# Routed expert blocks: up weights and tokens split into heads and remainders, loads three blocks ahead, result rows weighed by GpSimd in four buffers

## The chip, the core and the metric

The kernel runs on one core of a Trainium2 chip. Five engines work side by side and meet through semaphores: TensorE (PE) multiplies matrices and transposes, VectorE (DVE) and ScalarE (ACT) work on tiles, GpSimd (POOL) does both tile work and indirect transfers, SyncE (SP) issues the other transfers. Each engine takes its instructions in the order in which they are written. The metric is the device time in microseconds (us) of one execution, lower is better.

## What is computed

The input x has 4 x 512 tokens of 512 values. A state-space layer (a scan over 16 states for each channel, driven by a context) is gated and added to x. Then a mixture of experts follows: 2 shared experts for every token, and 16 routed experts of which each token takes the best 2.

```python
aff = jax.nn.sigmoid(jnp.einsum('bsd,de->bse', x, wa))
topk_p, topk_i = jax.lax.top_k(aff, K)                      # K = 2 of E = 16
topk_p = topk_p / jnp.sum(topk_p, axis=-1, keepdims=True)
combine = jnp.sum(jax.nn.one_hot(topk_i, E, dtype=x.dtype) * topk_p[..., None], axis=2)
# _experts_all: y = gelu(x @ g + gb) * (x @ w1 + b1); y @ w2 + b2     (D = 512, F = 256)
routed = jnp.einsum('bsed,bse->bsd', _experts_all(x, rg, rgb, rw1, rb1, rw2, rb2), combine)
shared = jnp.sum(_experts_all(x, sg, sgb, sw1, sb1, sw2, sb2), axis=2)
return x + shared + routed
```

## The kernel before

The first 480 us are the scan, then come gating, normalization, the shared experts and the routing. The change is in the last stage, the routed experts, from about 693 us on. There the 4096 pairs of a token and an expert have been sorted into `NBLK` = 47 blocks of 128 rows, each with rows of one expert alone. Block j belongs to expert `blk_e[j]`, its weights lie in slot `blk_slot[j]` of four, and `blk_load[j]` says whether they have to be loaded or are there already. `ids` and `row_w` hold the token and the weight of each row.

What happens to a block, in order, with the semaphore that each step raises:

- GpSimd fetches 128 rows of tokens (`fetch`, L534, xg_0 to xg_3). SyncE loads up weights (128 x 2048, 1 MB) and down weights (0.5 MB) into their slots (`load`, L366), two blocks ahead for up.
- TensorE transposes the tokens (L1550, xgt_ready); ScalarE copies them from PSUM to SBUF (L816, xgt_copied).
- TensorE multiplies by the up weights: four fp32 products of 512 columns, gate and linear half at once (L1559, h_ready). The trace has two rows of matmul for each.
- VectorE adds the bias (L1227, hb_ready), ScalarE applies gelu to one half (L820, hg_ready), VectorE multiplies the halves (L1233, hy_ready).
- TensorE transposes the result (L1567, hyt_ready), ScalarE copies it (L825), TensorE multiplies by the down weights (L1576, o_ready).
- VectorE adds the output bias (L1240, yb_ready), ScalarE weighs the rows (L831, `y_sb`, two buffers, y_ready), and GpSimd adds them to the output in DRAM by an indirect transfer (L560, y_even and y_odd when it has landed). Where a block starts a new expert, GpSimd first waits until the addition ahead of it has landed.

The steps of several blocks are interleaved by hand. `step(j)` on TensorE does up of j+1, transposed hidden of j, tokens of j+3, down of j-1; on VectorE bias j, product j, output bias j-2; on ScalarE gelu j, weighing j-2, transposed hidden j, tokens j+3. The steps of the first blocks and the last are written out, those between run in a hardware loop of four blocks. Where an operand depends on the expert or the slot, the engine first reads the number from SBUF into a register (`value_load`, TENSOR_LOAD in the order of instructions).

In the shared experts each fp32 operand is split already: a head rounded to the type fp32r and a remainder, and `split_product` (L1418 to L1420) makes three single-pass products for each pair of operands (head by head, head by remainder, remainder by head).

Results of the shared experts and x are added up in `acc`, and GpSimd stores its 16 tiles to the output (`store_base`, L523; early_stored for tiles 0 to 7, late_stored for 8 to 15) before the routed rows are added to them. `acc_again` is a name for the memory of `acc` that later steps may reuse; `mem` and `split` name one region in the same way.

## Time and profile before

| | before |
|---|---|
| median of 3 runs | 987.9 us (987.62 to 990.82) |
| profiled execution, time | 990.75 us |
| its span | 989.0 us |
| TensorE matmul, busy | 820.5 us, 83% of the span |
| TensorE weight load, busy | 562.8 us, 57% |
| VectorE, busy | 636.4 us, 64% |
| ScalarE, busy | 512.0 us, 52% |
| GpSimd, busy | 554.4 us, 56% |
| routed stage, first transpose to last up product | 693.4 to 962.6 us |

Busy shares are averages over stages with different limits: the scan keeps VectorE and GpSimd busy, the routed stage TensorE. Of the routed stage the reader should look at stretches of their own, and at which wait ends last there. Times below are counted from the start of the span.

### The profile page before, as it was taken

Reading aid. Unit: us, or ns where it says so; the run is one execution under the profiler, and the core shown is the slowest. Engines: PE = TensorE matmul, PEld = TensorE weight load, DVE = VectorE, ACT = ScalarE, POOL = GpSimd, SP = SyncE. Lnnn points to the kernel's source line nnn. Section 1 sums busy time; section 2 is a strip of 40 time slices with the busy share of each in tenths; the row PEclk is TensorE's granted clock in tenths of the full one; section 3 lists DMA queues with packets and bytes.
Section 4 is the critical chain, followed back from the end, with each engine's and each line's share of the span. In section 5 each row is a group of like instructions: output and inputs, shape, how many; then the busy total and the mean of one; then the engine's idle time right before and its main releaser. Section 6 shows DMA issues by size and latency. Waiting matters only on the chain.

```text
span 989.0 us, 14660 instructions
## 1 busy us (share of the span) xinstructions
PE 820.5 (83%) x4030; PEld 562.8 (57%) x4031; DVE 636.4 (64%) x669; ACT 512.0 (52%) x831; POOL 554.4 (56%) x483
## 2 busy tenths in 40 slices
PE   6987487677777777777588998989999999999991
PEld 2323476666666766666566776777445444544440
DVE  4858899989999998898877675542223332333230
ACT  3578498778888897898124321201233333333330
POOL 2211199889999899999555244020344444444331
PEclk9966699989999898998799998989999999999996
DMA  5010031112132112110311112046867877787533
GB/s 157 0 48 1 25 104 43 43 43 60 49 106 65 58 50 84 45 44 1 115 50 49 43 38 81 12 168 270 288 153 200 209 181 208 205 233 157 86 43 42
DMA packets 32421, 95.40 MB, mean 96 GB/s; under 512 B 5088, under 2 KB 5216, under 8 KB 29040
## 3 DMA queue, kind: packets, MB, share of 16 engines
q1 hardware_dynamic: 20400, 65.37, 19.4%
q0 software_dynamic: 11968, 29.37, 14.8%
q8 instruction: 28, 0.46, 0.2%
q14 instruction: 25, 0.20, 0.1%
HBM read 122.11 MB, written 21.36 MB: 145 GB/s over the span
## 4 chain that ended last, share of the span: by engine, by line
PE 59%; DVE 18%; issue 8%; POOL 7%; ACT 4%; DMA 2%; DVEq 0%; SPq 0%; POOLq 0%; ACTq 0%
PE ps L1559 16%; DVE r L953 11%; PE ps L1576 8%; POOL r L464 6%; PE ps L1364 5%; PE ps L1341 5%; PE ps L1418 5%; PE ps L1420 4%; PE ps L1419 4%; PE ps L1273 3%; PE ps L1550 2%; DVE r L962 2%; PE ps L1281 2%; PE ps L1296 1%; ACT mem L687 1%
## 5 line engine op out<-in xcount | busy, mean ns | idle before, releaser
L953 DVE TENSOR_TENSOR_SCAN r<-r,ps 128x1024 f32<-128x1024 f32 x128 | 286.0, 2271 | 24.2 <-PE ps L1364 15.5
L464 POOL TENSOR_TENSOR r<-r,mem 128x512 f32<-128x512 f32 x224 | 288.6, 1318 | 12.2 <-DVE r L953 6.8
L1341 PE MATMUL ps<-ident,mem 128*128 128x128 f32 x1024 | 145.5, 289 | 74.3 <-DVE r L953 56.7
L675 ACT ACTIVATE r<-mem,nega 128x511 f32<-128x511 f32 x256 | 168.7, 713 | 37.6 <-DVE r L953 37.6
L1341 PEld LDWEIGHTS ps<-ident,mem 128*128 128x128 f32 x1024 | 119.6, 148 | 97.5 <-issue 80.7
L1559 PE MATMUL ps<-r,mem 128*128 x376 | 169.1, 592 | 0.4 <-ACT mem L816 0.4
L1364 PE MATMUL ps<-ident,r 128*128 128x128 f32 x1024 | 145.3, 283 | 16.9 <-DVE r L962 10.4
L560 POOL DMA_INDIRECT out<-sg,ids x47 | 74.5, 1586 | 144.2 <-DMA out<-sg,ids 113.4
L1364 PEld LDWEIGHTS ps<-ident,r 128*128 128x128 f32 x1024 | 120.6, 145 | 25.1 <-DVE r L962 13.6
L687 ACT ACTIVATE mem<-mem,bc 128x512 f32<-128x512 f32 x192 | 124.7, 712 | 14.0 <-PE ps L1341 13.1
L1559 PEld LDWEIGHTS ps<-r,mem 128*128 128x128 f32 x376 | 71.2, 190 | 89.1 <-issue 89.1
L1227 DVE TENSOR_TENSOR mem<-ps,mem 128x512 f32<-128x512 f32 x47 | 32.5, 692 | 124.3 <-PE ps L1559 124.3
L1576 PE MATMUL ps<-mem 128*128 x188 | 88.5, 594 | 0.9 <-DVE sb_sb L1240 0.7
L1418 PE MATMUL ps<-split 128*128 128x512 f32 x192 | 78.5, 409 | 7.1 <-DVE split L1008 3.4
L831 ACT ACTIVATE sg<-sb_sb,row_w 128x512 f32<-128x512 f32 x47 | 33.9, 722 | 96.9 <-DVE sb_sb L1240 88.9
L456 POOL TENSOR_SCALAR mem<-mem,bc 128x512 f32<-128x512 f32 x64 | 53.7, 839 | 45.6 <-PE ps L1307 26.4
L1420 PE MATMUL ps<-split 128*128 128x512 f32 x192 | 76.4, 398 | 0.0
L1419 PE MATMUL ps<-split 128*128 128x512 f32 x192 | 76.3, 398 | 0.0
L748 ACT ACTIVATE sg<-ps,sbg_sb 128x512 f32<-128x512 f32 x16 | 11.0, 688 | 101.6 <-PE ps L1420 101.6
L534 POOL DMA_INDIRECT r<-xn_scratch,ids x47 | 48.6, 1034 | 24.0 <-issue 13.8
L825 ACT COPY mem<-ps 128x256 f32<-128x256 f32 x47 | 17.5, 372 | 79.2 <-PE ps L1567 73.0
L962 DVE TENSOR_TENSOR r<-r,mem 128x512 f32<-128x512 f32 x32 | 56.9, 1777 | 0.0
(172 smaller groups left out, 1000.8 us busy)
## 6 DMA issues: line engine op xcount, KB each, us to landing
r<-in_r_up SPq DMA_DIRECT2D x47, 1024.0 KB
mem<-in_r_down SPq DMA_DIRECT2D x47, 512.0 KB
mem<-cm_rows SPq DMA_DIRECT2D x64, 256.0 KB, 3.3
mem<-in_r_b SPq DMA_DIRECT2D x4, 2048.0 KB, 11.7
r<-in_x SPq DMA_DIRECT2D x4, 1024.0 KB, 4.9
xn_scratch<-r SPq DMA_DIRECT2D x16, 256.0 KB, 2.3
out<-acc POOLq DMA_DIRECT2D x16, 256.0 KB, 2.7
mem<-in_ctx_t SPq DMA_DIRECT2D x4, 512.0 KB, 8.3
```

Of the source, the lines that this page charges most:

```text
L464: pool.tensor_tensor(state[:, k % 2, ec], state[:, k % 2, ec], cb[:, k % CROWS], ALU.mult).then_inc(s["weighed_p"], 1)
L675: act.activation(decay[:, k % 2, ec, 1:L], delta[:, b, ec, 1:L], ACT.Exp, scale=nega[:, ec, n:n + 1]).then_inc(s["decay_ready"], 1)
L687: act.activation(dbu_t[:, k % 2, lt], du_t[:, t], ACT.Copy, scale=bc[:, t, DR + k % DS:DR + k % DS + 1]).then_inc(s["dbut_made_a"], 1)
L953: dve.tensor_tensor_scan(state[:, half, ec:ec + 2].rearrange("p e l -> p (e l)"), decay[:, half, ec:ec + 2].rearrange("p e l -> p (e l)"), ...
L962: dve.tensor_tensor(state[:, k % 2, EC - 1], state[:, k % 2, EC - 1], cb[:, k % CROWS], ALU.mult).then_inc(s["weighed_v"], 1)
L1341: mm = pe.transpose(ps[:, ec, lt * P:(lt + 1) * P], dbu_t[:, k % 2, lt, ec * P:(ec + 1) * P], ident[:])
L1364: mm = pe.matmul(ps[:, Y_BANK + lt, ec * P:(ec + 1) * P], state[:, k % 2, ec, lt * P:(lt + 1) * P], ident[:], is_transpose=True, start=Fal ...
L1418: pe.matmul(to, one_pass(l_head), one_pass(r_head), start=(first and i == 0), stop=False)
L1419: pe.matmul(to, one_pass(l_head), one_pass(r_rest), start=False, stop=False)
L1420: mm = pe.matmul(to, one_pass(l_rest), one_pass(r_head), start=False, stop=(last and i == n - 1))
L1559: mm = pe.matmul(ps[:, r % 2], xgt[:, r % 2, kc * P:(kc + 1) * P], up_weights(slot_j, kc), start=(kc == 0), stop=(kc == KC - 1))
L1576: mm = pe.matmul(ps[:, 6 + r % 2], hyt[:, r % 2, fc * P:(fc + 1) * P], down_weights(slot_j, fc), start=(fc == 0), stop=(fc == FC - 1))
```

## The change

Only the routed stage changes, in five places:

- ScalarE copies the up weights of each block from their slot to `up_head`, rounded (`weight_head`), and VectorE makes the remainder (`weight_rest`, a subtraction of 128 x 2048). The buffers, two of each, lie in `acc_again`.
- The transposed tokens are split likewise: ScalarE's copy is rounded, VectorE subtracts it from PSUM (`token_rest`).
- TensorE's `up` makes 12 single-pass products from the four parts instead of four fp32 ones. It waits for xgr_made and upr_made, VectorE's remainders.
- Up weights are loaded three blocks ahead (`AHEAD`), and a slot is free when its remainder is made, not when its product is.
- ScalarE's weighing is gone. VectorE writes the output bias sum straight into one of four buffers `y_sb`, and GpSimd multiplies it by `row_w` in place before its indirect addition. ScalarE's tokens come two blocks ahead instead of three.

```diff
+AHEAD = 3
-        xgt = view(mem, LATE_AT, 2, D)
+        xgt = view(split, LATE_AT, 2, D)
-        y_sb = sg
-        yb = sb2_sb
+        y_sb = (sg[:, 0], sg[:, 1], sb2_sb[:, 0], sb2_sb[:, 1])
+        up_head = view(acc_again, 0, 2, 2 * UP)[:, :, 0:UP]
+        up_rest = view(acc_again, 0, 2, 2 * UP)[:, :, UP:2 * UP]
+        xgt_rest = view(blk_val_again, 0, 2, D)
...
             def load_up(j, r):
                 if not isinstance(j, int) or j >= SLOTS:
-                    wait_apart(sp, s["h_ready"], j - SLOTS + 1)
+                    wait_apart(sp, s["upr_made"], j - SLOTS + 1)
...
                 for r in range(RING):
                     load_down(RING * jj + r, r)
-                    load_up(RING * jj + r + 2, (r + 2) % RING)
+                    load_up(RING * jj + r + AHEAD, (r + AHEAD) % RING)
...
-                pool.wait_ge(s["y_ready"], j + 1)
+                pool.wait_ge(s["yb_ready"], j + 1)
+                pool.tensor_scalar(y_sb[j % RING], y_sb[j % RING], row_w[:, j:j + 1], 1.0, ALU.mult, ALU.mult).then_inc(
+                    s["y_ready"], 1)
+                if j >= 2:
+                    pool.wait_ge(s["y_odd" if j % 2 else "y_even"], 16 * (j // 2))
...
             def turn_tokens(j, half):
                 act.wait_ge(s["xgt_ready"], j + 1)
                 since(act, s["h_ready"], j - 1)
-                act.copy(xgt[:, half], ps[:, 4 + half]).then_inc(s["xgt_copied"], 1)
+                act.copy(one_pass(xgt[:, half]), ps[:, 4 + half]).then_inc(s["xgt_copied"], 1)
+            def weight_head(j, r, round_):
+                slot_j = act.value_load(blk_slot[0:1, ds(j, 1)], min_val=0, max_val=SLOTS - 1)
+                act.wait_ge(s[f"up_{r}"], 16 * (round_ + 1))
+                since(act, s["h_ready"], j - 1)
+                act.copy(one_pass(up_head[:, r % 2]), up_weights(slot_j)).then_inc(s["uph_made"], 1)
...
             def step(j, round_, r):
+                if not isinstance(j, int) or j + 2 < NBLK:
+                    weight_head(j + 2, (r + 2) % RING, round_ + (r + 2) // RING)
+                    turn_tokens(j + 2, r % 2)
                 hidden_gate(j, r % 2)
-                if not isinstance(j, int) or j >= 2:
-                    block_result(j - 2, r % 2, (RING // 2) * round_ + (r - 2) // 2)
                 turn_hidden(j, r % 2)
-                if not isinstance(j, int) or j + 3 < NBLK:
-                    turn_tokens(j + 3, (r + 1) % 2)
+            act.wait_ge(s["blocks_ready"], 3)
+            act.wait_ge(s["early_stored"], 16 * NT // 2)
+            weight_head(0, 0, 0)
             act.wait_ge(s["so_ready"], NT)
             turn_tokens(0, 0)
             turn_tokens(1, 1)
-            turn_tokens(2, 0)
+            act.wait_ge(s["late_stored"], 16 * NT // 2)
+            weight_head(1, 1, 0)
...
-            add_shared(3, every)
+            def weight_rest(j, half):
+                slot_j = dve.value_load(blk_slot[0:1, ds(j, 1)], min_val=0, max_val=SLOTS - 1)
+                dve.wait_ge(s["uph_made"], j + 1)
+                dve.tensor_tensor(one_pass(up_rest[:, half]), up_weights(slot_j), up_head[:, half],
+                                  ALU.subtract).then_inc(s["upr_made"], 1)
+            def token_rest(j, half):
+                dve.wait_ge(s["xgt_copied"], j + 1)
+                dve.tensor_tensor(one_pass(xgt_rest[:, half]), ps[:, 4 + half], xgt[:, half],
+                                  ALU.subtract).then_inc(s["xgr_made"], 1)
...
-            def step(j, r):
+            def step(j, round_, r):
                 hidden_bias(j, r % 2)
+                if not isinstance(j, int) or 0 < j < NBLK - 1:
+                    token_rest(j + 1, (r + 1) % 2)
+                if not isinstance(j, int) or j >= 2:
+                    add_bias(j - 2, (r - 2) % RING, round_ + (r - 2) // RING)
                 hidden(j, r % 2)
-                if not isinstance(j, int) or j >= 2:
-                    add_bias(j - 2, r % 2)
+                if not isinstance(j, int) or j + 2 < NBLK:
+                    weight_rest(j + 2, r % 2)
+            weight_rest(0, 0)
+            add_shared(3, every)
+            token_rest(0, 0)
+            token_rest(1, 1)
+            weight_rest(1, 1)
...
-            def up(j, r, round_):
-                slot_j = pe.value_load(blk_slot[0:1, ds(j, 1)], min_val=0, max_val=SLOTS - 1)
-                pe.wait_ge(s["xgt_copied"], j + 1)
-                pe.wait_ge(s[f"up_{r}"], 16 * (round_ + 1))
+            def up(j, r):
+                pe.wait_ge(s["xgr_made"], j + 1)
+                pe.wait_ge(s["upr_made"], j + 1)
                 since(pe, s["hb_ready"], j - 1)
-                for kc in range(KC):
-                    mm = pe.matmul(ps[:, r % 2], xgt[:, r % 2, kc * P:(kc + 1) * P], up_weights(slot_j, kc),
-                                   start=(kc == 0), stop=(kc == KC - 1))
-                mm.then_inc(s["h_ready"], 1)
+                split_product(ps[:, r % 2], [(xgt[:, r % 2, kc * P:(kc + 1) * P], xgt_rest[:, r % 2, kc * P:(kc + 1) * P],
+                                              up_head[:, r % 2, kc * 2 * F:(kc + 1) * 2 * F],
+                                              up_rest[:, r % 2, kc * 2 * F:(kc + 1) * 2 * F])
+                                             for kc in range(KC)]).then_inc(s["h_ready"], 1)
```

How the order of instructions moves is shown at two places. The first is ScalarE in the loop of the routed blocks, one block before the change. L825 is the copy of the transposed hidden part, L816 the tokens, L820 the gelu, L831 the weighing; "waits" lists the semaphores.

```order
L820 ACTIVATE mem<-mem 128x256 [waits hb_ready]
L285 REGISTER_ALU [waits yb_ready]
L831 ISA [waits y_even]
L831 ACTIVATE sg<-sb_sb,row_w 128x512
L825 COPY mem<-ps 128x256 [waits o_ready,hyt_ready]
```

And the same place after it. Line numbers are those of the changed kernel: L831 is now the read of the slot number, L834 the weight heads, L827 the tokens, L838 the gelu, L843 the transposed hidden part.

```order
L831 ISA
L831 TENSOR_LOAD blk_slot
L831 ISA x2
L834 ISA [waits h_ready,up_3]
L834 COPY acc_again<-r 128x2048
L825 REGISTER_ALU
L827 CAST split<-ps 128x512 [waits h_ready,xgt_ready]
L838 ACTIVATE mem<-mem 128x256 [waits hb_ready]
L843 COPY mem<-ps 128x256 [waits o_ready,hyt_ready]
```

The weighing is gone; a read of the slot number and the copy of 2048 columns stand at the start of a block, behind the copy L843 of the block before and ahead of tokens and gelu.

The second place is VectorE in the same loop, one block before the change. L1227 is the bias, L1233 the product, L1240 the output bias; TENSOR_LOAD of `blk_e` reads the expert's number.

```order
L1227 ISA [waits hy_ready,hg_ready,h_ready]
L1227 TENSOR_TENSOR mem<-ps,mem 128x512
L1233 TENSOR_TENSOR mem<-mem 128x256 [waits hb_ready,hg_ready,hyt_ready]
L1218 TENSOR_LOAD blk_e
L1218 ISA x2
L1240 ISA [waits o_ready,y_ready]
L1240 TENSOR_TENSOR sb_sb<-ps,mem 128x512
```

After the change, in its line numbers, L1249 is the bias, L1241 the token remainder, L1263 the output bias, L1255 the product and L1236 the weight remainder.

```order
L1249 ISA [waits hy_ready,hg_ready,h_ready]
L1249 TENSOR_TENSOR mem<-ps,mem 128x512
L1241 TENSOR_TENSOR blk_val_again<-ps,split 128x512 [waits xgt_copied]
L1230 TENSOR_LOAD blk_e
L1230 ISA x2
L1263 ISA [waits y_odd,o_ready]
L1263 TENSOR_TENSOR sg<-ps,mem 128x512
L1255 TENSOR_TENSOR mem<-mem 128x256 [waits hb_ready,hg_ready,hyt_ready]
L1234 ISA
L1234 TENSOR_LOAD blk_slot
L1234 ISA x2
L1236 ISA [waits uph_made]
L1236 TENSOR_TENSOR acc_again<-r,acc_again 128x2048
```

The token remainder stands behind the bias, the output bias has moved ahead of the product, and a third read of a register and the weight remainder stand behind the product.

## Rows read from the trace of the kernel before

**Rows 1.** Chain that ended last, routed stage: start us, us, what.
```profile
698.58 0.44 PE ps L1550 x4
...
703.40 3.60 DMA r<-xn_scratch,ids
...
709.88 3.43 PE ps L1559 x8
...
713.31 0.22 PE ps L1567 x2
...
959.16 3.45 PE ps L1559 x8
...
967.75 4.60 DMA out<-sg,ids
```

**Rows 2.** Busy time by stretch; the last three columns: TensorE clock, DMA share, GB/s.
```profile
680.00:685.00 5.00, 3.92 (x12) 2.83 (x11) 1.63 (x3) 0.62 (x1) 0.59 (x1) 0.73 0.99 419
...
850.00:900.00 50.00, 50.00 (x158) 25.00 (x157) 15.35 (x26) 17.20 (x35) 24.63 (x19) 1.00 0.82 215
```

**Rows 3.** Timeline of one routed block: start us, us, engine, line, operation.
```profile
800.26 0.38 PE L1567 MATMUL ps<-ident,mem 128*128 128x128 f32 x2
...
800.68 0.37 ACT L825 COPY mem<-ps 128x256 f32<-128x256 f32 x1 [1.62 <-PE ps L1567]
...
801.19 0.58 ACT L816 COPY mem<-ps 128x512 f32<-128x512 f32 x1
...
801.67 0.42 ACT L820 ACTIVATE mem<-mem 128x256 f32<-128x256 f32 x1
...
802.18 0.43 DVE L1233 TENSOR_TENSOR mem<-mem 128x256 f32<-128x256 f32 x1 [0.90 <-ACT mem L820]
...
803.04 0.69 DVE L1240 TENSOR_TENSOR sb_sb<-ps,mem 128x512 f32<-128x512 f32 x1 [0.43 <-issue]
...
813.72 0.48 DVE L1233 TENSOR_TENSOR mem<-mem 128x256 f32<-128x256 f32 x1 [0.68 <-ACT mem L820]
...
814.92 0.69 DVE L1240 TENSOR_TENSOR sb_sb<-ps,mem 128x512 f32<-128x512 f32 x1 [0.72 <-PE ps L1576]
```

**Rows 4.** Timeline of TensorE in the shared experts, single-pass products.
```profile
672.02 0.39 PE L1418 MATMUL ps<-split 128*128 128x512 f32 x1
...
674.74 0.39 PE L1418 MATMUL ps<-split 128*128 128x512 f32 x1
...
679.63 0.50 PE L1418 MATMUL ps<-split 128*128 128x512 f32 x1 [0.65 <-DVE split L1014]
...
679.97 0.39 PE L1419 MATMUL ps<-split 128*128 128x512 f32 x1
```

**Rows 5.** Timeline of VectorE: subtractions and products of 2048 columns, remainders of 512.
```profile
104.55 2.28 DVE L885 TENSOR_TENSOR mem<-mem,r 128x2048 f32<-128x2048 f32 x1
...
106.75 1.27 DVE L919 COPY mem<-ps 128x512 f32<-128x512 f32 x2
...
530.09 2.48 DVE L1008 TENSOR_TENSOR split<-ps,split 128x512 fp32r<-128x512 f32 x4 [0.46 <-ACT split L741]
```

**Rows 6.** Groups by line and shape, ScalarE and GpSimd: count, busy us, mean ns.
```profile
L635 ACT ACTIVATE r<-r 128x2048 f32<-128x2048 f32 x4 | 7.7, 1919 | 1.7 <-DVE r L879 1.7
...
L456 POOL TENSOR_SCALAR mem<-mem,bc 128x512 f32<-128x512 f32 x64 | 53.7, 839 | 45.6 <-PE ps L1307 26.4 <-PE ps L1341 19.2
```

**Rows 7.** Timelines of GpSimd and VectorE in the scan, two long operations.
```profile
97.65 4.83 POOL L456 TENSOR_SCALAR mem<-mem,bc 128x512 f32<-128x512 f32 x1
...
170.05 5.40 DVE L962 TENSOR_TENSOR r<-r,mem 128x512 f32<-128x512 f32 x1
```

**Rows 8.** Timeline of GpSimd, its fifth fetch.
```profile
703.40 0.99 POOL L534 DMA_INDIRECT r<-xn_scratch,ids  x1 [9.41 <-PE ps L1550]
```

**Rows 9.** DMA queues, 693.5 to 702.6 us: packets, MB, share.
```profile
q0 software_dynamic: 201, 0.63, 17.2%
```

**Rows 10.** DMA queues, 702.6 to 704.9 us.
```profile
q1 hardware_dynamic: 106, 0.84, 92.1%
```

More of the change, by code:

```diff
@@ L219, in bass_xattn_scan_moe_kernel @@
         row_hot = view(r0, 8192, 2, GROUP, P)
-        blk_val = sb("blk_val", [P, 2, GROUP, 2 * NBLK])
+        with ExitStack() as listing:
+            blk_val = listing.enter_context(nc.sbuf_tensor("blk_val", [P, 2, GROUP, 2 * NBLK], F32))
+        blk_val_again = sb("blk_val_again", [P, 2 * GROUP * 2 * NBLK])
         half_i = sb("half_i", [P, 2 * ((NBLK + 3) // 2)], I32)
@@ L286, in wait_apart, with up_weights @@
             eng.sem_inc(S["waits_passed"], 1)
[L288 to L290 removed]
+        def up_weights(slot_j):
+            return up_w[:, bass.ds(slot_j, 1)].rearrange("p o n -> p (o n)")
         def down_weights(slot_j, fc):
@@ L390, in _ @@
             sp.dma_start(b2_all[:, 0:E // 2], r_b2[0:E // 2].unsqueeze(0).to_broadcast([P, E // 2, D])).then_inc(s["loaded_b2"], 16)
-            for j in range(2, RING):
-                load_up(j + 2, (j + 2) % RING)
+            for j in range(1, RING):
+                load_up(j + AHEAD, (j + AHEAD) % RING)
             with sp.Fori(1, (NBLK - 2) // RING) as jj:
@@ L852, in _ @@
                 step(j, j // RING, j % RING)
-            for j in range(NBLK - 2, NBLK):
-                block_result(j, j % 2, j // 2)
         @block.vector
@@ L1547, in turn_tokens @@
                 pe.wait_ge(s[f"xg_{r}"], 16 * (round_ + 1))
-                since(pe, s["xgt_copied"], j - 1)
+                since(pe, s["xgr_made"], j - 1)
                 for kc in range(KC):
@@ L1590, in _ @@
             turn_tokens(1, 1, 0)
-            up(0, 0, 0)
+            up(0, 0)
             turn_tokens(2, 2, 0)
@@ L1600, in _ @@
             last = NBLK - 1
-            up(last, last % RING, last // RING)
+            up(last, last % RING)
             turn_hidden(last - 1, (last - 1) % RING)
```

37 lines of the change are left out of this document (16 added, 21 removed).

## The prediction

> **What bounds the kernel now.** I read the chain that ended last first. From 713 us on it is TensorE alone: up products (L1559), transposes (L1567, L1550), down products (L1576), block after block, with no wait between them [rows 1]. Call E(j) the moment at which the up products of block j end, which is where the transposes behind them start. E(3) is 713.31; the last up products, of block 46, start at 959.16 and take 3.45, so E(46) is 962.61 [rows 1]. That is 249.3 us for 43 blocks, 5.80 us each. In 850 to 900 us TensorE is busy for all of the stretch at the full clock, while VectorE works 31%, ScalarE 34% and GpSimd 49% of it [rows 2]. So anything that shortens TensorE's work in a block is gained, until another engine or a loop through several engines is longer than TensorE's work.
>
> **TensorE's share of the change.** Up goes from 3.43 us of fp32 products [rows 1] to 12 single-pass products. The same form runs in the shared experts: from 672.02 to 674.74 are twelve of them, 2.72 us, 0.227 each at the full clock [rows 4]. That takes 0.71 off, and TensorE's work in a block becomes 5.80 - 0.71 = 5.09 us.
>
> **What it adds elsewhere, per block.** ScalarE copies 2048 columns of weights: the nearest rows are four activations of the same shape, 1.92 us [rows 6]; it loses the 0.72 us of weighing. VectorE subtracts the same 2048 columns, 2.28 us as at 104.55 [rows 5], and 512 columns of tokens from PSUM, 0.69 or less: four such operations in a row took 2.48 us [rows 5]. VectorE's busy time is then 3 x 0.69 + 0.43 + 2.28 = 4.78 us, ScalarE's 1.92 + 0.58 + 0.42 + 0.37 = 3.29. Both are under 5.09, so by busy time alone nothing stands against a gain of 0.71 us a block. GpSimd gets the weighing, 0.84 us by the mean of its like, L456 [rows 6], and has the room. Loading three blocks ahead costs nothing: a slot is free once the remainders are made, and four blocks of lead hold either way.
>
> **The loop that busy time doesn't show.** The new steps stand in series through four engines. ScalarE works in program order: transposed hidden of block j-1, weight heads of j+2, tokens of j+2, gelu of j. VectorE: bias j, token remainder j+1, output bias j-2, hidden product j, weight remainder j+2. TensorE's up of block j+2 waits for the token remainder of j+2, which stands behind bias j+1, which stands behind the weight remainder of j+2. Followed from E(j), with starts read from one block [rows 3]:
> - transposes end, ScalarE starts its copy: 800.26 to 800.68, 0.42
> - that copy's start to the weight heads. A slot number has to be read into a register in between, and the order of instructions shows the read behind the copy. ScalarE has no such read before the change; VectorE has one between L1233 and L1240, and there the starts lie 0.86 (802.18, 803.04) to 1.20 (813.72, 814.92) apart [rows 3]. I take 0.95
> - weight heads: 1.92 [rows 6] less the 0.1 by which ScalarE's operations overlap (801.19 + 0.58 against 801.67 [rows 3]): 1.80 rounded
> - tokens to gelu 0.48, gelu to hidden product 0.51 [rows 3]
> - hidden product to weight remainder, again with a read of the slot, 0.95
> - weight remainder to the next VectorE operation: 104.55 to 106.75, 2.20 [rows 5]
> - bias j+1 0.60 and token remainder 0.68, from the pace of the four [rows 5]
> - TensorE starts 0.05 after it; the first product after a wait takes 0.34 instead of 0.23 (679.63 to 679.97) [rows 4], then the rest of 2.72: 2.88
>
> The sum is 11.47 us from E(j) to E(j+2), so 5.74 us a block, although no engine works more than 5.09. With the reads at 0.86 it is 5.65, at 1.20 5.99. So of the 0.71 us that TensorE saves, 0.06 is left. In the change the weighing went to GpSimd, whose operation starts when output bias j-2 ends. That is about 3.5 us after E(j), and it reaches into the start of hidden product j at about 4.1. I allow 0.1 us a loop for that.
>
> The Trainium skill (VectorE: DVE Perf Modes, The DRAIN you can't avoid) says that the next VectorE operation doesn't start until the pipe is empty. Here it starts 0.08 us before the end of the one ahead (104.55 + 2.28 against 106.75) [rows 5], so the trace disagrees; by that rule the three back-to-back steps of the loop would be 0.25 us longer and a block 0.12.
>
> **The start.** The weights' heads and remainders lie where the result rows lay, and the second half of it may be written only when the last eight tiles of rows are stored. GpSimd waits for the same stores ahead of its fifth fetch, which starts at 703.40 [rows 8]; its queue still had 201 packets between 693.5 and 702.6 [rows 9], and from there to 704.9 only SyncE's queue had any [rows 10]. So the stores land at about 702.6. Now ScalarE waits for them before the heads of block 1. From there: heads 703.5 to 705.4, remainder to 707.7, up of block 1 from 707.8. TensorE has then been idle since the transposes of block 2, about 699.0 [rows 1]. After shorter pauses the clock was at 0.73 in 680 to 685, against 1.00 later [rows 2]: part of that stretch ran at 1.2 GHz. I take eight products at half the clock, so up takes 4.3 us and E(1) is 712.1. One loop on, E(3) is 723.6 instead of 713.31: 10.3 us lost. Before, this stretch had a stall of its own (3.60 us for a fetch at 703.40 [rows 1]), which is in the 713.31.
>
> **The sum.** E(45) = 723.6 + 21 x 11.47 = 964.5. The even blocks run by a loop of their own: weight remainder of 2 to 712.2, bias 1 at 712.4, token remainder to 713.7, E(2) = 716.6, and E(46) = 716.6 + 22 x 11.47 = 968.9, at least 5.09 behind E(45): 969.6. With 0.1 a loop for the weighing 971.8. That is 9.2 later than 962.61. Behind E(46) the result of block 44 waits for ScalarE no longer; I take off 0.5 and no more, since the last additions to the output each wait for the landing of the one ahead, 4.60 us at 967.75 [rows 1], either way. So +8.7 us. The profiled execution took 990.75 us (span 989.0), 2.85 over the median of 987.9. It would become 999.4, the median 996.6. I say 996.
>
> **Rivals.**
> - TensorE stays the bound (0.10). The reads of registers overlap or ScalarE runs ahead, and the loop is under 10.2 us. For it: both engines are idle half of the time. Against it: the sum above, which would have to be 1.3 us too long. E(46) = 723.6 + 43 x 5.09 = 942.5, 20 us earlier; median 967.
> - The loop is 10.6 to 11.2 us, or the start costs less (stores earlier, clock not lowered) (0.21). E(46) lies between 952 and 964: median 977 to 990, half of it under 985.
> - The shared port (0.16). GpSimd and VectorE shut each other out: a weighing-like operation of GpSimd (L456) took 4.83 us at 97.65, beside VectorE's operations with two SBUF inputs, and a 512-column product of VectorE (L962) took 5.40 at 170.05, beside GpSimd [rows 7]. The rule behind it is in the Trainium skill (GPSIMD Engine Reference, Key points): contention with VectorE instructions that have two SBUF inputs. Hidden product and weight remainder are such, the other three read PSUM. If each loop waits once for a whole 0.84, a block costs (11.47 + 0.84) / 2 = 6.16 us, and E(46) is 723.6 + 43 x 6.16 = 988.5, 26 later; median 1013; for half of that wait 1004. It decides from 0.1 us a loop on.
> - The forecast (0.53): 991 to 1003.
>
> **How the numbers follow.** No change is told from one here only beyond 0.3%, 3 us. Faster than 985: the first rival and half of the second, 0.20. Within 3 us: the rest of the second, 0.11, and the low edge of the forecast, 0.02. Slower 0.67. The range leaves out most of the first rival and the top of the third: 978 to 1011.
>
> **What the changed profile would show.** Twelve products of 0.23 us for a block; TensorE idle about 0.6 us ahead of each up, released by VectorE's token remainder; ScalarE's heads of 1.9 us about 1.4 us after E(j); VectorE's weight remainder about 4.9 after it; E(3) near 723 and an idle stretch of 8 us ahead of up 1. I am wrong if TensorE shows no idle time (first rival), if the gap between hidden product and weight remainder is under 0.3 us, if weight remainders take over 2.6 or hidden products over 0.6 (third), or if the heads of block 1 start well before 703.

## The result, and the profile after

The changed kernel takes 1023.4 us (median of four executions) against 987.8 before: 1.034 times as long, 95% interval 1.025 to 1.042. (The ratios in this document compare means and leave out executions of a slower state that turns up now and then, here the one of 1033.64 us.) The forecast was 996, the range 978 to 1011. The profiled execution after took 1020.27 us, its span is 1018.4. The parts ahead of the routed stage, whose code the change leaves alone, come out differently from one execution to the next: the last addition to a base row (L1029 before, L1041 after) starts at 692.47 us before and at 684.43 after, and between 683 and 705 us in the kernels below. The difference is there when the scan ends, near 470 to 490 us, and it goes mostly with one group: the scan's 32 products of VectorE (`r<-r,mem`, 128x512, the L962 of [rows 7]) take 1.45 us in the mean after, 1.78 before, and 2.19 to 2.22 in the three kernels below in which that addition comes last, behind 701 us. The order is not strict: in gate_first it is 1.86 us with the addition at 685.9. Why the products take so long in some executions is open. So profiles are compared here by three parts of the routed stage, read from the timeline: **start**, from the start of that last addition to E(3); **blocks**, E(3) to E(46); **tail**, E(46) to the end of the span. E(j) is the start of the transposes behind the up products of block j, as in the prediction.

```
                          start    blocks (each)    tail   stage
before                     20.7    249.3 (5.80)     26.6   296.5
predicted                  31.1    248.2 (5.77)     26.1   305.4
after                      31.7    259.4 (6.03)     42.8   334.0
```

The stage is 37.5 us longer, of which the prediction had 8.9 (8.7 in its own sum, where E(46) of before is read 0.2 later). Its start was right, the blocks are 11 us longer than forecast, the tail 17.

**Start**, timeline of the kernel after (columns as in [rows 3]; of the lines in between these are the ones that matter), then windows of it (columns as in [rows 2]):

```profile
684.43 0.69 DVE L1041 TENSOR_TENSOR acc<-ps,acc 128x512 f32<-128x512 f32 x1 [2.03 <-PE ps L1452]
...
695.63 3.70 ACT L834 CAST acc_again<-r 128x2048 fp32r x2 [8.46 <-DMA out<-acc]
...
697.67 2.29 DVE L1236 TENSOR_TENSOR acc_again<-r,acc_again 128x2048 fp32r<-128x2048 f32 x1 [9.66 <-ACT acc_again L834]
...
700.11 0.77 PE L1450 MATMUL ps<-acc_again,split 128*128 128x512 f32 x1 [7.59 <-DVE acc_again L1236]
...
705.10 0.38 PE L1598 MATMUL ps<-ident,mem 128*128 128x128 f32 x2
```

```profile
700.00:705.00 5.00, 4.89 (x12) 3.92 (x13) 3.28 (x3) 0.42 (x1) 0.78 (x1) 0.52 0.19 52
```

ScalarE's heads of block 1 wait 8.46 us for the stores (`out<-acc`), VectorE's remainder waits for the heads, TensorE 7.59 us for the remainder. This is the chain of the prediction: the heads start 11.2 us behind the start of the last base addition, where 11.0 was forecast. Up of block 1 then takes 5.0 us (700.11 to 705.10) instead of the 4.3 I took. The granted clock is 0.52 in 700 to 705, so nearly all of the stretch runs at 1.2 GHz: the first eleven products start 0.42 to 0.56 us apart, where 0.23 is the distance at 2.4 GHz.

**Blocks.** These are the starts of TensorE's transposes, E(3) to E(7):

```profile
716.15 0.38 PE L1598 MATMUL ps<-ident,mem 128*128 128x128 f32 x2
721.29 0.38 PE L1598 MATMUL ps<-ident,mem 128*128 128x128 f32 x2
727.63 0.38 PE L1598 MATMUL ps<-ident,mem 128*128 128x128 f32 x2
732.79 0.38 PE L1598 MATMUL ps<-ident,mem 128*128 128x128 f32 x2
739.32 0.38 PE L1598 MATMUL ps<-ident,mem 128*128 128x128 f32 x2
```

Two blocks take 11.48, then 11.50, then 11.69 us, so the loop of 11.47 is there, but the pace doesn't stay. The next lines are waits of TensorE and VectorE in 715 to 975 us (us in total, times, longest):

```profile
PEld ps L1450 <- DVE blk_val_again L1241: 50.9, 43, 2.0
...
DVE sg L1263 <- DMA out<-sg,ids: 8.8, 7, 3.9
...
DVE sb_sb L1263 <- DMA out<-sb_sb,ids: 7.8, 5, 2.6
```

The first is the loop's wait for token remainders. The other two are new: VectorE's output bias of block j waits until the addition of block j-4 has landed, 16.6 us in all. The longest of these waits belong to one stall: an addition took 10.81 us from issue to landing, and GpSimd and then VectorE waited (the first line is from the chain, the second from the timeline).

```profile
839.53 10.81 DMA out<-sb_sb,ids
...
859.14 0.69 DVE L1263 TENSOR_TENSOR sg<-ps,mem 128x512 f32<-128x512 f32 x1 [3.86 <-DMA out<-sg,ids]
```

The three blocks from E(25), 845.14, to E(28), 867.95, take 22.8 us, and the other forty 5.92 each. So about 5 of the 11 us over the forecast were lost here. The other 6 are spread over all blocks. The chain that ended last, in 730 to 940 us, was TensorE alone before [rows 1]; now it holds no TensorE at all:

```profile
by line: issue 30.9%; DMA out<-sb_sb,ids 21.0%; POOL r L540 18.3%; POOL sg L560 8.7%; POOL out L571 8.4%; POOL sb_sb L560 6.1%; DMA out<-sg,ids 5.2%; POOLq L568 2.2%; POOLq L292 0.5%
```

It is GpSimd's chain: scaling (L560), register read (L568), addition (L571) and its landing, fetch (L540). Here is one round of it on the timeline, with VectorE's weight remainder (L1236) beside it:

```profile
820.01 0.85 POOL L560 TENSOR_SCALAR sg<-sg,row_w 128x512 f32<-128x512 f32 x1
820.88 2.29 DVE L1236 TENSOR_TENSOR acc_again<-r,acc_again 128x2048 fp32r<-128x2048 f32 x1 [0.58 <-issue]
821.71 2.96 POOL L571 DMA_INDIRECT out<-sg,ids  x1 [0.84 <-POOL sg L560]
824.98 1.01 POOL L540 DMA_INDIRECT r<-xn_scratch,ids  x1 [0.30 <-issue]
...
826.01 0.85 POOL L560 TENSOR_SCALAR sg<-sg,row_w 128x512 f32<-128x512 f32 x1
826.41 2.60 DVE L1236 TENSOR_TENSOR acc_again<-r,acc_again 128x2048 fp32r<-128x2048 f32 x1
827.70 2.80 POOL L571 DMA_INDIRECT out<-sg,ids  x1 [0.84 <-POOL sg L560]
```

From addition to addition it takes 5.99 us: 2.96 + 0.30 + 1.01 + 0.02 + 0.85 + 0.84 (times and idle times, in order), and no wait for a landing is in it. An addition took 1.59 us before (mean of 34 in 750 to 950 us). Here it is 2.96, and it ends at 824.67, 1.50 behind the end of the remainder at 823.17; the next one ends at 830.50, 1.49 behind the end of the remainder at 829.01. This is no accident of two. Between E(3) and E(46) eleven additions start 0.11 us or more into a remainder. They take from 1.91 to 3.69 us, and every one ends 1.50 us behind the end of the remainder, nearly the whole length of an addition that is left alone. In the same way 16 fetches end 0.88 to 0.89 us behind it, and eleven scalings 0.54 to 0.56. Additions that start ahead of a remainder take 1.60 to 1.86. So an instruction of GpSimd that starts under a remainder does next to nothing until VectorE has finished. The groups of GpSimd's instructions in 750 to 950 us (busy us, mean ns | idle before, releaser):

```profile
L540 POOL DMA_INDIRECT r<-xn_scratch,ids x31 | 49.2, 1587 | 9.5 <-issue 9.2 <-DMA out<-sg,ids 0.3
L571 POOL DMA_INDIRECT out<-sb_sb,ids x16 | 32.8, 2053 | 20.0 <-POOL sb_sb L560 9.6 <-DMA out<-sb_sb,ids 7.6 <-DMA out<-sg,ids 2.9
L571 POOL DMA_INDIRECT out<-sg,ids x16 | 32.4, 2023 | 20.6 <-POOL sg L560 11.0 <-DMA out<-sb_sb,ids 8.5 <-issue 1.0
L560 POOL TENSOR_SCALAR sg<-sg,row_w 128x512 f32<-128x512 f32 x16 | 20.4, 1273 | 0.6
L560 POOL TENSOR_SCALAR sb_sb<-sb_sb,row_w 128x512 f32<-128x512 f32 x16 | 16.1, 1006 | 0.6
```

**Tail.** This is the same chain from E(46), 975.59, on:

```profile
978.85 5.10 DMA out<-sg,ids
...
984.84 4.79 DMA out<-sb_sb,ids
...
990.52 4.94 DMA out<-sb_sb,ids
...
996.36 4.83 DMA out<-sg,ids
...
1002.08 4.67 DMA out<-sg,ids
...
1007.65 1.59 POOL out L571
```

Six additions are issued behind E(46), each waiting for the landing of the one ahead, 5.6 to 6.0 us apart. Before there were three, the first at 967.75 [rows 1], and one more that started with E(46) itself, at 962.45. Three more additions at 5.6 us or more are about the 16 us by which the tail is longer. GpSimd was three blocks behind when TensorE ended.

### The profile page after: what moved, and what is told of

Read it like the earlier page. It is cut to its first block, busy times and chain, and to the rows that moved or that the text cites. A ratio compares the mean times of both kernels' runs of the same rounds, so it can differ in the third digit from the quotient of the medians.

```text
span 1018.4 us, 15319 instructions
## 1 busy us (share of the span) xinstructions
PE 808.2 (79%) x4218; PEld 591.9 (58%) x4219; DVE 761.9 (75%) x763; ACT 563.0 (55%) x832; POOL 648.3 (64%) x530
## 4 chain that ended last, share of the span: by engine, by line
PE 33%; DVE 18%; POOL 16%; issue 15%; DMA 12%; ACT 4%; POOLq 1%; DVEq 0%; SPq 0%; ACTq 0%
DVE r L965 11%; DMA out<-sb_sb,ids 6%; POOL r L470 5%; PE ps L1373 5%; PE ps L1450 5%; DMA out<-sg,ids 5%; PE ps L1396 5%; PE ps L1451 5%; PE ps L1452 5%; POOL r L540 4%; PE ps L1305 2%; POOL out L571 2%; POOL sg L560 2%; PE ps L1313 2%; PE ps L1328 1%
## 5 line engine op out<-in xcount | busy, mean ns | idle before, releaser
L1373 PE MATMUL ps<-ident,mem 128*128 128x128 f32 x1024 | 141.1, 283 | 72.7 <-DVE r L965 51.2
L1373 PEld LDWEIGHTS ps<-ident,mem 128*128 128x128 f32 x1024 | 115.5, 145 | 95.8 <-issue 70.1
L1236 DVE TENSOR_TENSOR acc_again<-r,acc_again 128x2048 fp32r<-128x2048 f32 x47 | 110.7, 2356 | 29.6 <-issue 18.1
L834 ACT CAST acc_again<-r 128x2048 fp32r x47 | 89.2, 1901 | 36.5 <-issue 28.1
L1450 PE MATMUL ps<-acc_again,split 128*128 128x512 f32 x188 | 81.8, 435 | 28.1 <-DVE blk_val_again L1241 20.2
L1607 PE MATMUL ps<-mem 128*128 x188 | 93.2, 621 | 3.5 <-ACT mem L843 3.4
L540 POOL DMA_INDIRECT r<-xn_scratch,ids x47 | 70.8, 1507 | 32.1 <-issue 13.2
L843 ACT COPY mem<-ps 128x256 f32<-128x256 f32 x47 | 17.5, 372 | 111.9 <-PE ps L1598 108.2
L1450 PEld LDWEIGHTS ps<-acc_again,split 128*128 128x128 f32 x188 | 36.3, 193 | 68.9 <-DVE blk_val_again L1241 54.7
L1452 PE MATMUL ps<-acc_again,blk_val_again 128*128 128x512 f32 x188 | 75.5, 402 | 0.0
L1451 PE MATMUL ps<-acc_again,split 128*128 128x512 f32 x188 | 75.4, 401 | 0.0
L571 POOL DMA_INDIRECT out<-sg,ids x24 | 48.0, 2001 | 41.8 <-DMA out<-sb_sb,ids 16.5
```

Source lines behind the costliest of these rows:

```text
L540: pool.indirect_dma_start(out=xg[:, j % RING], out_offset=None, in_=xn_dram, in_offset=bass.IndirectOffsetOnAxis(ids[:, j:j + 1], 0)).then ...
L1236: dve.tensor_tensor(one_pass(up_rest[:, half]), up_weights(slot_j), up_head[:, half], ALU.subtract).then_inc(s["upr_made"], 1)
L1373: mm = pe.transpose(ps[:, ec, lt * P:(lt + 1) * P], dbu_t[:, k % 2, lt, ec * P:(ec + 1) * P], ident[:])
L1450: pe.matmul(to, one_pass(l_head), one_pass(r_head), start=(first and i == 0), stop=False)
L1451: pe.matmul(to, one_pass(l_head), one_pass(r_rest), start=False, stop=False)
L1452: mm = pe.matmul(to, one_pass(l_rest), one_pass(r_head), start=False, stop=(last and i == n - 1))
```

## Experiments

The experiments set two theories against each other. Theory A: GpSimd's work for a block, made longer by the scaling and stretched by VectorE, has become the bound (A1: the stretching decides; A2: four steps in series are too long without it). Theory B: the loop through the other three engines is 6.0 by itself. The table has the three parts of each profile, and the times. Each ratio is to the kernel before as it ran beside that experiment (medians of 990.1 to 992.9 us), so kernels of different groups are compared by the ratio and not by the time.

```
kernel        start   blocks (each)   tail   stage   time, median   ratio to before (95%)
after_again    32.2   257.4 (5.99)    43.2   332.8    1020.2        1.032  (1.025-1.039)
act_weighs     32.2   253.1 (5.89)    27.8   313.1    1008.0        1.015  (1.009-1.021)
rest_psum      31.8   245.5 (5.71)    26.8   304.0    1001.5        1.012  (1.006-1.019)
fold           32.2   250.7 (5.83)    26.2   309.1    1013.1        1.021  (1.016-1.026)
weigh_only     21.5   249.3 (5.80)    27.2   298.0     991.0        1.002  (0.997-1.007)
gate_first     31.6   255.1 (5.93)    40.0   326.7    1028.4        1.038  (1.029-1.047)
start_fix      22.8   255.9 (5.95)    42.6   321.3    1015.6        1.023  (1.016-1.031)
best1          23.7   250.4 (5.82)    26.0   300.1     994.1        1.002  (0.999-1.005)
best2          22.6   243.9 (5.67)    28.6   295.1     987.6        0.992  (0.988-0.997)
best3          22.7   238.6 (5.55)    28.8   290.0     988.5        0.993  (0.987-0.998)
best4          22.9   232.6 (5.41)    29.3   284.8     980.8        0.992  (0.989-0.996)
best5          22.5   232.8 (5.41)    39.5   294.8     992.7        1.002  (0.997-1.006)
```

**after_again**, no edit.

> The changed kernel once more, nothing edited, as the measure for the three beside it. Every theory expects 1015 to 1027 us. In its trace the stage should again be made of three parts: about 31 us from the last addition to a base row (L1029's) to E(3), the moment at which the up products of block 3 end; about 6.0 us a block from E(3) to E(46); and some 40 us or more from E(46) to the end, with about six additions to the output issued behind E(46).

All three parts came again within 2 us. Each part is read from one profiled execution, so differences of 2 us between kernels are not told apart here.

**act_weighs**

```diff
-                pool.tensor_scalar(y_sb[j % RING], y_sb[j % RING], row_w[:, j:j + 1], 1.0, ALU.mult, ALU.mult).then_inc(
+                act.activation(y_sb[r], y_sb[r], ACT.Copy, scale=row_w[:, ds(j, 1)]).then_inc(s["y_ready"], 1)
```

> The changed kernel with the weighing back on ScalarE, in the same four buffers; nothing else. Theory A (GpSimd's serial work for a block, scaling, register read, addition, fetch, about 6 us, is longer than the loop through the other engines): without the scaling GpSimd needs 4.7 us, the blocks fall to the loop's 5.75, only three additions stand behind E(46), the tail is 25 to 30 us. Time 997 to 1006. Theory B (the loop through ScalarE, VectorE and TensorE is 6.0 by itself, GpSimd only follows): blocks stay at 6.0, 1008 to 1016 with a shorter tail at most. Theory C (the four buffers or loads three ahead do the harm): no change, 1015 to 1027.

The tail is back at 27.8 us, as theory A has it, but a block takes 5.89, 0.14 longer than it said, and the time of 1008.0 lies above its range and at the edge of theory B's. Theory B had room for a shorter tail, so this run alone doesn't decide between the two; the next one does. Theory C falls: the four buffers and the loads three ahead were kept.

**rest_psum**

```diff
-                dve.tensor_tensor(one_pass(up_rest[:, half]), up_weights(slot_j), up_head[:, half],
-                                  ALU.subtract).then_inc(s["upr_made"], 1)
+                    dve.tensor_tensor(one_pass(up_rest[:, half]).rearrange("p (c n) -> p c n", c=KC),
+                                      up_head[:, half].rearrange("p (c n) -> p c n", c=KC),
+                                      ps[:, 4 + half, 0:UP // KC].unsqueeze(1).to_broadcast([P, KC, UP // KC]),
+                                      ALU.subtract).then_inc(s["upr_made"], 1)
```

> The changed kernel, but from block 2 on the weights' remainder is computed with the second operand read from PSUM (a 512-column bank, read four times) in place of the loaded weights in SBUF: as many columns, one SBUF input instead of two. The remainders are then wrong in value. Theory A1 (GpSimd's instructions are stretched because VectorE's operation with two SBUF inputs shuts it out): scalings fall from a mean of 1.27 us to about 0.85, fetches from 1.57 to about 1.05, additions from 1.98 to about 1.6, GpSimd's work in a block to under 5 us, time 995 to 1006 with a tail under 32. Theory A2 (GpSimd is too long only because four steps stand in series, and the port has no part): all durations on GpSimd stay within 0.1, time 1015 to 1027.

The kernel still has the scaling on GpSimd, and VectorE's operation takes 2.29 us. These are its groups on GpSimd, same stretch and columns:

```profile
L540 POOL DMA_INDIRECT r<-xn_scratch,ids x34 | 34.4, 1012 | 10.4 <-issue 10.1 <-DMA out<-sg,ids 0.3
L571 POOL DMA_INDIRECT out<-sg,ids x18 | 29.2, 1624 | 33.3 <-DMA out<-sb_sb,ids 16.6 <-DMA out<-sg,ids 8.0 <-POOL sg L560 6.0
...
L560 POOL TENSOR_SCALAR sb_sb<-sb_sb,row_w 128x512 f32<-128x512 f32 x18 | 13.0, 724 | 7.3 <-DVE sb_sb L1269 6.8
```

The fetch goes from 1.59 to 1.01, the addition from 2.04 to 1.62, the scaling from 1.14 to 0.72 (means over both buffers): 1.4 us a block less on GpSimd, from one input of a VectorE operation. No addition takes over 1.67 us, wherever it starts. The tail is 26.8, the scaling now waits for VectorE, and no VectorE operation waits for a landing. A1 holds, A2 falls. So does theory B: the loop through the other three engines has the same steps here, and it isn't 6.0. With GpSimd out of the way a block takes 5.71 us, and the prediction's sum for the loop was 5.74. The Trainium skill (GPSIMD Engine Reference, Key points) has the rule behind it, contention with VectorE instructions that have two SBUF inputs. The trace agrees, and it shows the same for the instructions with which GpSimd issues indirect transfers.

**fold**

```diff
+                dve.scalar_tensor_tensor(out=hy[:, half], in0=hg[:, half], scalar=row_w[:, ds(j, 1)],
+                                         in1=hb[:, half, F:2 * F], op0=ALU.mult, op1=ALU.mult).then_inc(s["hy_ready"], 1)
...
+                dve.scalar_tensor_tensor(out=y_sb[r], in0=tile(b2_all, e), scalar=row_w[:, ds(j, 1)],
+                                         in1=ps[:, 6 + r % 2], op0=ALU.mult, op1=ALU.add).then_inc(s["yb_ready"], 1)
```

> The changed kernel, with the weighing folded into two VectorE operations of the same length: the hidden product also takes the row's weight, and the output bias is taken times that weight, so that no engine has a weighing of its own and GpSimd has only fetches and additions. Theory A (GpSimd's chain): 996 to 1005, blocks at 5.7 to 5.8 us, tail 25 to 30 us, the additions and fetches still stretched beside the weights' remainder. Theory B (loop of the other three is 6.0 by itself): 1008 to 1016. If fused operations of VectorE with a scalar from SBUF are slower than the plain ones by 0.2 us each, a block is 0.2 longer, and it is 1005 to 1012.

No engine has a weighing of its own, the tail is 26.2 and a block 5.83. The fused operations take 0.06 us longer than the plain ones, 0.484 and 0.743 against 0.426 and 0.686 in act_weighs (means in 750 to 950 us), not 0.2. The time, 1013, is above the 996 to 1005 expected. The stage (309.1) is 13 us over that of before, and the rest lies ahead of it, where this kernel has the code of the others. Against after_again the stage is 24 us shorter and the time only 7.

**weigh_only**, the kernel before with GpSimd's lines of the change.

```diff
-                act.activation(y_sb[:, half], yb[:, half], ACT.Copy, scale=row_w[:, ds(j, 1)])
+                pool.tensor_scalar(y_sb[j % RING], y_sb[j % RING], row_w[:, j:j + 1], 1.0, ALU.mult, ALU.mult).then_inc(
```

> The kernel before, with only the weighing moved to GpSimd and the result in four buffers; up products in fp32 as before, no heads and no remainders. Theory A1 (GpSimd's work becomes too long because VectorE's weight remainder shuts it out): without the remainder GpSimd's scaling takes about 0.72 us, its addition 1.6, its fetch 1.05, under 5 us with the register read, so TensorE stays the bound at 5.80 us a block, and the time is that of before, 985 to 994. Theory A2 (the scaling in series is too much by itself): blocks of 5.9 to 6.1 us and a tail of 35 us or more, 1000 to 1015.

A1 again: the time is the same within the interval, and blocks take 5.80. (Its profiled execution was 13 us over its median, 12 of them ahead of the stage.) So the scaling is harmless alone; it takes the weight remainder beside it.

**gate_first**

```diff
+                hidden_gate(j, r % 2)
                 if not isinstance(j, int) or j + 2 < NBLK:
                     weight_head(j + 2, (r + 2) % RING, round_ + (r + 2) // RING)
                     turn_tokens(j + 2, r % 2)
-                hidden_gate(j, r % 2)
```

> The changed kernel, but ScalarE does the gelu of block j ahead of the weight heads and tokens of block j+2 instead of behind them. By the sum of the prediction that takes about 1.1 us off the loop of two blocks (10.2 to 10.4 us in place of 11.47). Theory A (GpSimd's work for a block, stretched, is 5.9 to 6.1 us and is the bound): blocks stay at 5.8 to 6.0 us, and what is won from E(3) to E(46) comes back in a longer tail; time 1010 to 1024. Theory B (the loop through ScalarE, VectorE and TensorE is the bound and GpSimd only follows it): blocks at 5.2 to 5.4 us and 990 to 1000.

A block takes 5.93 us and the tail 40, as theory A has it; the time of 1028.4 is above its range. There is a second reason why the blocks did not get shorter, see best1.

**start_fix**

```diff
             turn_tokens(1, 1)
-            act.wait_ge(s["late_stored"], 16 * NT // 2)
-            weight_head(1, 1, 0)
...
+                    if isinstance(j, int) and j == 1:
+                        act.wait_ge(s["late_stored"], 16 * NT // 2)
                     weight_head(j + 2, (r + 2) % RING, round_ + (r + 2) // RING)
...
+                    for kc in range(KC):
+                        mm = pe.matmul(ps[:, r % 2], y_sb[3][:, kc * P:(kc + 1) * P],
+                                       up_weights(slot_j)[:, kc * 2 * F:(kc + 1) * 2 * F],
+                                       start=(kc == 0), stop=(kc == KC - 1))
```

> The changed kernel, but block 1 alone is multiplied in fp32 as before the change, from a full copy of its tokens, so that no weight head or remainder of it is made, and ScalarE waits for the last stores of the rows only ahead of the head of block 3. The prediction's start term (about 10 us lost because heads of block 1 wait for the late stores): the time from the last addition to a base row to E(3) falls from 31 us to 20 to 22, the rest stays, time 1010 to 1017. If the start is lost to something else (the fetch of block 4 behind the same stores, or a low clock): it falls by less than 3 us, time 1017 to 1024.

The start falls by 8.9 us, to 22.8 where 20 to 22 was expected, and the time of 1015.6 is in the range. So the start term is shown: the wait of block 1's heads for the stores costs 9 of the 11 us.

**best1**: fold, gate_first and start_fix together, and the fetch of block 4 no longer waits for the stores.

> Four edits together: weighing folded into VectorE's two operations, gelu ahead of the weight heads on ScalarE, block 1 in fp32, and GpSimd waits for the stores of the rows only ahead of the first addition, so that the fetch of block 4 does not wait for them. If GpSimd without the scaling keeps up (theory A), the start is 18 to 21 us, a block 5.2 to 5.5 us, the tail 26 to 30: 962 to 977. If GpSimd's stretched fetch and addition or the landing of additions still bind at 5.7 to 5.8: 982 to 990.

Theory A's 5.2 to 5.5 us a block did not come, and 994.1 us is above both ranges. The timeline shows a loop I had not worked out (rows of VectorE and ScalarE, block after block the same):

```profile
799.87 2.29 DVE L1239 TENSOR_TENSOR acc_again<-r,acc_again 128x2048 fp32r<-128x2048 f32 x1 [1.29 <-ACT acc_again L837]
...
802.08 0.68 DVE L1253 TENSOR_TENSOR mem<-ps,mem 128x512 f32<-128x512 f32 x1
...
802.79 0.42 ACT L841 ACTIVATE mem<-mem 128x256 f32<-128x256 f32 x1 [1.32 <-DVE mem L1253]
...
803.56 1.91 ACT L837 CAST acc_again<-r 128x2048 fp32r x1 [0.35 <-issue]
...
805.62 2.29 DVE L1239 TENSOR_TENSOR acc_again<-r,acc_again 128x2048 fp32r<-128x2048 f32 x1 [1.15 <-ACT acc_again L837]
```

With the gelu ahead, the heads of block j+2 wait for the bias of block j, which stands behind the weight remainder of j+1: one block per turn, 5.75 us. So the "about 1.1 us off the loop" expected for gate_first was wrong. The two orders come out alike, 5.82 a block here and 5.83 in fold, which has the order of the change.

**best2**: best1 with ScalarE's order of the change again, and

```diff
                 hidden_gate(j, r % 2)
+                if more:
+                    slot_j = slot_of(j + 3)
                 turn_hidden(j, r % 2)
...
+                if more:
+                    slot_j = slot_of(j + 2)
                 hidden(j, r % 2)
```

> As the kernel of four edits, but ScalarE's order is that of the change again (weight heads ahead of the gelu), and the slot number is read into a register earlier: on ScalarE ahead of the wait for the transposed hidden rows, on VectorE ahead of the hidden product. The prediction's loop of two blocks loses the two reads that it counts (about 0.45 us each of the 0.95 steps): 10.5 to 10.7 us, 5.25 to 5.35 a block. If the loop bounds: E(3) to E(46) 226 to 232 us, start 21 to 23, tail 26 to 29, time 966 to 975. If GpSimd (fetch, register read, addition, stretched) bounds at 5.7 or more: 245 to 250 from E(3) to E(46) or a tail over 35, 985 to 992.

Early pairs of blocks take 10.5 to 10.6 us as expected, but the mean of a block is 5.67, and the time of 987.6 misses the 966 to 975. In the chain, 740 to 752 us, SyncE's queue (SPq) has taken over (L369 to L372 are 52% of it in the whole loop, 716 to 948 us):

```profile
by line: issue 25.1%; SPq L369 21.6%; SPq L370 21.1%; SPq L372 15.7%; SPq L371 15.3%; SPq L403 1.1%; SPq L292 0.6%
```

Its issues of weight loads in the timeline:

```profile
742.14 0.36 SPq L372 DMA_DIRECT2D mem<-in_r_down  x1
745.59 0.35 SPq L372 DMA_DIRECT2D r<-in_r_up  x1
748.11 0.09 SPq L372 DMA_DIRECT2D mem<-in_r_down  x1
750.59 0.09 SPq L372 DMA_DIRECT2D r<-in_r_up  x1
```

It takes 2.5 to 3.5 us from load to load, and a block has two loads. L369 to L371 read expert, "new or not" and slot into registers; that is most of it.

**best3**: best2, heads and remainder of a block in two halves of 1024 columns.

> As the one above, and the weights of a block are split in two halves of 1024 columns, so that VectorE's first half of the remainder runs beside ScalarE's second half of the heads. The loop loses another 0.95 us less two short overheads of 0.1 to 0.2: 9.7 to 9.9 us, so that TensorE's own work (5.09 us and some 0.1 of restart) becomes the bound: 5.1 to 5.25 a block, 219 to 226 us from E(3) to E(46), time 958 to 970. If GpSimd bounds, no gain over the one above, and a longer tail.

The stage is 5 us shorter and the time no different. E(3) to E(46) takes 238.6 us where 219 to 226 was expected, and the time of 988.5 is far above the 958 to 970. SyncE's reads and the landing of additions are in the chain.

**best4** and **best5**: best3 and best2, with SyncE reading the numbers of a block once for both loads. With it the up weights are loaded two blocks ahead again, and ahead of the down weights.

```diff
+                        known.append(numbers(j + 2))
+                        load_up(j + 2, (r + 2) % RING, known[r + 2])
+                    load_down(j, r, known[r])
-                    load_down(RING * jj + r, r)
-                    load_up(RING * jj + r + AHEAD, (r + AHEAD) % RING)
```

> As the kernel with early reads and halves, but SyncE reads the three numbers of a block (expert, new or not, slot) once for its two loads, up two blocks ahead, instead of once for each load; at the start of each round of four it reads two blocks again, so 18 reads in four blocks instead of 24. In the two kernels ahead SyncE issues its two loads of a block 5.3 to 5.8 us apart, one after the other without a wait. If SyncE's reads bound them: blocks fall from 5.55 to 5.15 to 5.3 us, 222 to 228 from E(3) to E(46), time 968 to 980. If the additions, which land some 5.5 us after their issue and wait for each other, are the bound: 235 to 240 as before, or a tail longer by what is gained, 984 to 992.

> The same edit of SyncE on the kernel with early reads, without halves. If SyncE's reads bound that one: 226 to 230 from E(3) to E(46) (the loop of 5.25 to 5.35 us), time 972 to 982. If the additions bound: 240 to 245 as before, 984 to 992.

Both fall in blocks, to 5.41: 6.0 us less than best3, 11.1 less than best2, so SyncE's reads did bound them. Both are still up to 0.1 us a block above the expected range, which is left open, and the times are above theirs, by 1 us in best4 and 11 in best5. For best5 gives all that it gains back in the tail. The next lines are GpSimd's fetches and additions, best4 first, then best5:

```profile
L560 POOL DMA_INDIRECT r<-xn_scratch,ids x34 | 39.5, 1163 | 10.4 <-issue 8.8 <-DMA out<-sb_sb,ids 0.6 <-DMA out<-sg,ids 0.6
L589 POOL DMA_INDIRECT out<-sb_sb,ids x19 | 34.6, 1821 | 45.8 <-DMA out<-sg,ids 24.8 <-DMA out<-sb_sb,ids 16.4 <-issue 4.6
```

```profile
L560 POOL DMA_INDIRECT r<-xn_scratch,ids x32 | 50.2, 1569 | 9.8 <-issue 7.9 <-DMA out<-sb_sb,ids 0.9 <-DVE sb_sb L1293 0.9
L589 POOL DMA_INDIRECT out<-sb_sb,ids x17 | 37.5, 2203 | 31.5 <-DMA out<-sg,ids 13.6 <-DMA out<-sb_sb,ids 10.6 <-DVE sb_sb L1293 4.6
```

The kernels differ only in whether heads and remainder are one operation each (VectorE's of 2.29 us) or two (of 1.22). With one, a fetch is stretched to 1.57 us, and six additions stand behind E(46); with two it is 1.16, and four do. best4 has the shortest stage, 284.8 us, and takes 0.992 (0.989 to 0.996) of before; best2 and best3 come out at the same ratio.

## Why the prediction was wrong, step by step

- **Twelve products of 0.23, the loop, 11.47 us.** This was right. Early pairs took 11.48 to 11.69, and rest_psum, with GpSimd out of the way, runs at 5.71 a block against 5.74.
- **The start, 10.3 us.** This was right: 11.0 measured, and start_fix takes 8.9 of them back. Up of block 1 was 0.7 longer than I took. Of that 0.2 is a slip in the sum, since eight products at half the clock and four at the full one are 8 x 0.454 + 4 x 0.227 = 4.5 us and not 4.3; the rest is that nearly all ran at the lower clock.
- **"GpSimd gets the weighing, 0.84 us by the mean of its like, L456 [rows 6], and has the room."** This step failed, and with it the sum: GpSimd's round was priced at nothing. I had GpSimd's busy share from [rows 2] (49%), and left out what lies between its instructions: 0.84 us from scaling to addition, 0.30 to the fetch, and landings. 1.06 + 0.30 + 1.59 + 0.84 + 0.72 is 4.5 us at the lengths without contention, which would have fitted (weigh_only, rest_psum). Stretched under the weight remainder it is 6.0, more than the 5.74 of the loop. So GpSimd falls behind until VectorE waits for its additions, which gives blocks of 6.03 and three more additions in the tail: 11.2 and 16.7 us over the forecast, of the 28.6 that the stage is over it.
- **The shared port.** It was the right rival with the wrong victim. I priced one wait of 0.84 us a loop on the scaling or the hidden product, 1013 us in all. What is stretched is all that GpSimd does: the fetch by 0.58 in the mean, addition and scaling by 0.42 each, and single additions by 2.1 (to 3.69), since the remainder of 2.29 us lies over one of them in nearly every block. The signs that the prediction named for this rival came only in part: remainders took 2.36 us in the mean and 2.77 at most, hidden products 0.53 in the mean and 1.02 at most. The rows at hand showed 5 us stalls between the two engines [rows 7], and I tried them only on the instruction that the change moved, not on those already there.
- **The tail, "I take off 0.5 and no more, since the last additions to the output each wait for the landing of the one ahead".** The landings behind one another were right, and they are what made the backlog dear: GpSimd came to E(46) three additions further behind, each 5.6 us or more, and the tail is 16.2 us longer than before. I had assumed that the backlog is the same in both kernels.
- **"I allow 0.1 us a loop for that."** Two blocks took 12.07 us in the mean where 11.57 was forecast, so the loop came out 0.6 longer than its 11.47 and not 0.1. Of these 0.6 about 0.24 is the one stall behind the addition at 839.53 (5 us in 21.5 loops). The delay of the hidden product by the scaling, for which the 0.1 stood, is there: it starts 0.80 us behind the gelu in the mean of E(3) to E(46), and 0.51 in rest_psum.
- **The pipe that has to be empty.** The prediction sets a sentence of the Trainium skill (VectorE: DVE Perf Modes, The DRAIN you can't avoid) against the rows. The same section adds that an operation which is not held starts earlier, so the 0.08 us of overlap don't contradict it. In the kernel after, too, bias starts 2.21 us behind the start of a remainder of 2.29.

Taking the scaling off GpSimd (act_weighs, fold) is enough to bring the tail back; that leaves the start and blocks of 5.8 to 5.9, 13 to 17 us over before in the stage. The split itself gains nothing on this loop, as forecast. A block still takes 0.12 us longer in fold and 0.18 in act_weighs than in rest_psum. Part of it lies ahead of the weight remainder, where VectorE idles 0.55, 0.60 and 0.38 us in the three (means in 750 to 950 us, released by no wait that the profile shows). Why is left open; fold and act_weighs keep the operation with two SBUF inputs.

## What to carry to other kernels

When work is moved to an engine that is half idle, add up its whole round for one block in series, with register reads, gaps and landings, and then stretch every instruction in it, old ones too, to the end of the longest operation with two SBUF inputs that VectorE may run beside it. An engine that falls behind by a fraction of a block every time shows up at the end: count what it has still to issue when the bound engine stops. And after each bound that is removed, work the loop out anew; behind GpSimd there stood the loop with the register reads of ScalarE and VectorE, then the six reads of SyncE, then in best5 GpSimd again.

## What the runs showed of the hardware

- GpSimd's indirect transfers take longer to issue while VectorE runs an operation with two SBUF inputs: fetches 1.01 to 1.59 us, additions 1.62 to 2.04 in the mean (rest_psum against after), single ones to 3.13 and 3.69. Each that starts 0.11 us or more into VectorE's operation ends 1.50 us (addition) or 0.88 us (fetch) behind it. A VectorE operation of the same columns with one input from PSUM takes 2.29 us as well and stretches nothing (no addition over 1.67).
- Two operations of 1.22 us do less harm than one of 2.29: fetches of 1.16 us against 1.57, and four additions behind E(46) against six (best4, best5).
- A load whose address and condition come from three registers costs SyncE 2.5 to 3.5 us, and two such loads a block bounded best2 at 5.67 us a block.
- TensorE's twelve single-pass products after 7.6 us of idling took 5.0 us instead of 2.7: the granted clock was 0.50 in 695 to 700 and 0.52 in 700 to 705, that is 1.2 GHz nearly throughout, and 1.00 in 705 to 706.
